# A transformer and RWKV layer stack on one core: the loading block ahead of batch 0 is dissolved into the main block

## The reference

```python
x = x + attn_a(_layernorm(x), Wq, Wk, Wv, Wo)      # 16 heads of 16, rotary, causal softmax
x = x + ffn(_layernorm(x), w_gate, w_up, w_down)   # weights int32 / 127, hidden 768
x = x + attn_b(_layernorm(x), maa_*, Wr, Wk, ...)  # 4 heads of 64, state S = w*S + k v
x = x + ffn(_layernorm(x), w_gate, w_up, w_down)
```

## Time and profile before

| | us |
|---|---|
| median of 3 runs | 3376.86 (3376.3 to 3377.62) |
| profiled execution, its own time | 3373.62 |
| span of the profiled execution | 3371.8 |
| TensorE matmul busy | 2943.3 (87%) |
| VectorE busy | 2399.7 (71%) |
| ACT, GpSimd busy | 1311.6 (39%), 1413.6 (42%) |
| granted TensorE clock, mean | 0.960 |

### The profile page before, as it was taken

One profiled execution on the slowest core, in us unless ns is written; L12 is line 12 of the kernel. 1 busy time (PEld: TensorE's weight loads), 2 busy tenths in 40 slices (PEclk: granted clock), 3 DMA queues, 4 the chain that ended last, 5 costly groups with the idle time before them and its releaser, 6 DMA issues.

```text
span 3371.8 us, 47013 instructions
## 1 busy us (share of the span) xinstructions
PE 2943.3 (87%) x17088; PEld 1831.6 (54%) x17088; DVE 2399.7 (71%) x4593; ACT 1311.6 (39%) x2721; POOL 1413.6 (42%) x1596
## 2 busy tenths in 40 slices
PE   2398989989899898999989998898988989899898
PEld 1135565365653666445763457635575365654567
DVE  4485687767877677866778658785587756876666
ACT  0164314723246323453225532364313733247222
POOL 0123462335623356234552336423463334623454
PEclk9699999999999999999999999999999999999999
DMA  3700024000340004300051002500024000240000
GB/s 132 129 2 1 19 39 96 2 1 19 46 89 2 1 19 69 66 2 10 17 89 39 1 10 41 102 2 2 19 39 96 2 1 19 39 84 2 1 1 14
DMA packets 70610, 114.96 MB, mean 34 GB/s; under 512 B 9451, under 2 KB 62731, under 8 KB 64187
## 3 DMA queue, kind: packets, MB, share of 16 engines
q1 hardware_dynamic: 67091, 110.72, 16.8%
q10 hardware_dynamic: 3264, 0.79, 0.1%
HBM read 74.69 MB, written 33.65 MB: 32 GB/s over the span
## 4 chain that ended last, share of the span: by engine, by line
PE 51%; DVE 23%; POOL 12%; issue 5%; ACT 3%; DMA 3%; SPq 0%; DVEq 0%; POOLq 0%; ACTq 0%
PE PB L1411 7%; PE PB L1395 6%; PE PB L1381 6%; PE PB L1483 5%; PE PB L1468 5%; DVE mxp L1073 4%; DVE arena L1250 4%; PE PB L1420 3%; PE PB L1525 3%; DVE arena L1259 3%; DVE attn L995 2%; PE PB L1560 2%; POOL hl L683 2%; PE PB L1550 2%; DMA arena<-augT 2%
## 5 line engine op out<-in xcount | busy, mean ns | idle before, releaser
L1073 DVE TENSOR_REDUCE mxp<-PB 128x1 f32<-128x512 f32 (+3 forms) x1216 | 723.5, 652 | 149.3 <-PE PB L1384 96.1
L826 ACT ACTIVATE arena<-PB 128x512 f32<-128x512 f32 (+3 forms) x1536 | 657.6, 512 | 408.6 <-PE PB L1395 358.5
L1381 PE MATMUL PB<-arena 96*128 96x512 bf16 (+3 forms) x1536 | 463.2, 343 | 49.4 <-DMA arena<-parts 31.5
L1395 PE MATMUL PB<-arena 99*128 99x512 bf16 (+3 forms) x1536 | 444.1, 336 | 45.1 <-DMA arena<-augT 25.6
L683 POOL TENSOR_TENSOR hl<-arena,hh 128x512 fp32r<-128x512 f32 x192 | 251.8, 1311 | 357.0 <-ACT hh L853 354.0
L1468 PE MATMUL PB<-xh,wgu 128*128 128x512 f32 x768 | 317.1, 413 | 34.0 <-DVE xl L1126 18.4
L1411 PE MATMUL PB<-arena 128*32 128x512 f32 (+3 forms) x3072 | 325.6, 498 | 9.6 <-POOL arena L659 9.6
L1468 PE MATMUL PB<-xl,wgu 128*128 128x512 f32 x768 | 310.0, 404 | 0.6 <-issue 0.6
L1381 PEld LDWEIGHTS PB<-arena 96*128 96x128 bf16 x1536 | 151.6, 100 | 281.0 <-DVE mxp L1073 96.3
L659 POOL TENSOR_SCALAR_AFFINE_SELECT arena<-arena 128x512 f32<-128x512 f32 x256 | 162.4, 635 | 330.8 <-ACT arena L826 304.0
L703 POOL TENSOR_TENSOR arena<-arena,xT 128x512 f32<-128x512 f32 x160 | 184.2, 1175 | 261.8 <-DVE arena L1192 261.8
(11 more groups left out here) (142 smaller groups left out, 5531.1 us busy)
## 6 DMA issues: line engine op xcount, KB each, us to landing
arena<-parts SPq DMA_DIRECT2D x112, 256.0 KB, 9.5
parts<-arena SPq DMA_DIRECT2D x192, 128.0 KB
arena<-parts SPq DMA_DIRECT2D x16, 768.0 KB, 17.4
arena<-in_x SPq DMA_DIRECT2D x16, 512.0 KB, 7.0
arena<-parts SPq DMA_DIRECT2D x16, 512.0 KB, 19.6
xres<-in_x SPq DMA_DIRECT2D x16, 512.0 KB, 4.6
out<-xres SPq DMA_DIRECT2D x16, 512.0 KB, 14.0
wgu<-arena SPq DMA_DIRECT2D x2, 768.0 KB, 4.5
```

Of the source, the lines that this page charges most:

```text
L826: act.activation(pt[:, U % 3, h, 0:n], bank(b, "score", t)[:, 0:n], ACT.Exp, scale=DH ** -0.5).then_inc(act_emptied, 1)
L1073: dve.reduce_max(mxp[:, k // 2 % 2, hs[0]:hs[-1] + 1, col:col + 1], bank(b, "max", t)[:, 0:n * len(hs)].rearrange("p (h n) -> p h n", n=n) ...
L1381: last = mm(ps, qst[0:AUG, i // 4, HG * (k // 2) + h, 128 * (i % 4):128 * (i % 4) + 128], kst[0:AUG, s0 // HALF, HG * (k // 2) + h, 0:n], ...
L1395: mm(ps[:, 0:n], kst[0:AUG + 3, j // 4, h, 128 * (j % 4):128 * (j % 4) + 128], qst[0:AUG + 3, f, h, HALF - n:HALF], start=True, stop=True) ...
```

## The change

There is one block now. SP's order in it: x of batch 0; ident and the q, k, v weights (s_qkv); the rotary tables (s_rope); the three integer matrices and the causal mask (s_ints), now at HIGH in the arena; ones_dram; the parts stores and stack loads of batch 0; then the moves of the feed-forward weights (s_raw), wo in 4 pieces, all other weights (s_w, NLOAD 23 loads); the width row; then as before. GpSimd's memsets stand ahead of its first scale. TensorE waits for s_qkv ahead of its first transpose, and for s_cast (causal and identb) ahead of batch 0's steps. VectorE waits for s_rope ahead of the rotary part; behind the last split of the head it casts the masks and the integers, in place and in three parts, and checks the width part by part, cast, comparison (`not_equal` in place of a subtraction and a comparison with zero) and maximum. ACT waits for s_raw ahead of batch 0's exponentials and their augT DMAs. The flag is made on VectorE behind the third joined maximum of batch 0 and loaded by TensorE at O_STEP. What reads the late weights waits for s_w once, in batch 0.

```diff
-        with nc.Block() as block:
-            @block.sync
...
-                dve.tensor_copy(identb[:, :], ident[:, :]).then_inc(s_cast, 1)
...
+        NW = NC * HID
+        whole = [region(HIGH + NW * k, NW) for k in range(3)]
+        wide_at = rounded("wide_at", HIGH + 3 * NW, [128, 1, NW])
+        wide_col = region(HIGH + 12800, 4)
...
                 x0_in(0)
+                sp.dma_start(ident[:, :], consts[0][:, 0:128]).then_inc(s_qkv, 16)
+                for k, w in enumerate(w_at[0:3]):
+                    sp.dma_start(wqkv[:, :, D * k:D * k + D], w.rearrange("(c p) n -> p c n", p=128)).then_inc(s_qkv, 16)
+                for k in (0, 1):
+                    sp.dma_start(rope[:, k, :], cs[k]).then_inc(s_rope, 16)
...
+                sp.wait_ge(s_zero, NZERO)
+                sp.dma_start(ones_dram, ones).then_inc(s_ones, 16)
                 parts_store(0, range(4))
                 stack_loads(sp, 0, 0)
                 parts_store(0, range(4, 8))
+                sp.wait_ge(s_ones, 16)
                 stack_loads(sp, 0, 1)
+                sp.wait_ge(s_whole, 3)
+                for k in (0, 1):
+                    sp.dma_start(wgu[:, :, HID * k:HID * k + HID].bitcast(f32),
+                                 whole[k].rearrange("p (c n) -> p c n", c=NC)).then_inc(s_raw, 16)
+                sp.dma_start(wd[:, :, :].bitcast(f32), whole[2].rearrange("p (m n) -> p m n", m=NM)).then_inc(s_raw, 16)
...
+                sp.wait_ge(s_wide, 10)
+                sp.dma_start(wide_row[0:1, :], wide_col[:, 3:4]).then_inc(s_flag, 16)
...
+                    if b == 0:
+                        act.wait_ge(s_raw, 48)
                     for t in range(NSC):
...
+                dve.wait_ge(s_rope, 32)
                 for e in (0, 2, 4, 6):
                     pair(rotary, 0, e)
                     pair(remainder, 0, e)
                     pair(low, 0, e)
+                dve.wait_ge(s_ints, 64)
+                dve.wait_ge(s_qkv, 64)
+                dve.tensor_copy(causal[:, :], causal_in)
+                dve.tensor_copy(identb[:, :], ident[:, :]).then_inc(s_cast, 1)
+                for k in range(3):
+                    dve.tensor_copy(whole[k], whole[k].bitcast(i32)).then_inc(s_whole, 1)
+                dve.wait_ge(s_whole, 3)
+                w_ = wide_at[:, 0, :]
+                for k in range(3):
+                    if k:
+                        dve.wait_ge(s_wide, 3 * k)
+                    dve.tensor_copy(w_, whole[k]).then_inc(s_wide, 1)
+                    dve.wait_ge(s_wide, 3 * k + 1)
+                    dve.tensor_tensor(w_.bitcast(f32), whole[k], w_.bitcast(f32), ALU.not_equal).then_inc(s_wide, 1)
+                    dve.wait_ge(s_wide, 3 * k + 2)
+                    dve.reduce_max(wide_col[:, k:k + 1], w_.bitcast(f32), axis=AX.X).then_inc(s_wide, 1)
...
+                        if b == 0 and t == BLOCK_END[5]:
+                            dve.wait_ge(s_flag, 16)
+                            dve.reduce_max(wide_row[0:1, 0:1], wide_row[0:1, :], axis=AX.X).then_inc(s_wide, 1)
+                            dve.wait_ge(s_wide, 11)
+                            dve.tensor_copy(wide_flag[0:1, :], wide_row[0:1, 0:1]).then_inc(s_wide, 1)
+                            dve.wait_ge(s_w, 16 * NLOAD)
+                            dve.wait_ge(s_zero, NZERO)
...
-                pe.reg_load(wide, wide_flag[0:1, 0:1])
...
+                pe.wait_ge(s_qkv, 64)
                 for f in (0, 1):
                     transpose_x0(0, f)
...
+                    if b == 0:
+                        pe.wait_ge(s_cast, 1)
                     for t in range(STEPS):
+                        if b == 0 and t == O_STEP:
+                            pe.wait_ge(s_w, 16 * NLOAD)
+                            pe.wait_ge(s_wide, 12)
+                            pe.wait_ge(s_raw, 48)
+                            pe.reg_load(wide, wide_flag[0:1, 0:1])
```

137 lines of the change are left out of this document (55 added, 82 removed).

## The result

| | before | changed |
|---|---|---|
| median, us | 3377.11 (3376.3 to 3377.62) | 3338.73 (3336.75 to 3340.49, 4 runs) |
| profiled execution: span, own time | 3371.8, 3373.62 | 3338.7, 3340.49 |
| first score matmul (L1395, now L1410) | 155.42 | 115.53 |
| from there to the end of the span | 3216.4 | 3223.2 |
| granted clock, mean | 0.960 | 0.957 |

The ratio of the medians is 0.9886 (95% interval 0.9869 to 0.9904): the change saves 38.4 us. The forecast was 3332.4, range 3324 to 3346: sign and range hold, and some 6 us of the forecast gain of 44.5 did not come. The two profiled executions do not stand at the medians: the one before took 3373.62, 3.5 less than its median, and the changed one 3340.49, 1.8 more. So the spans differ by less (33.1) than the medians do (38.4).

What follows compares the result with a forecast made beforehand. It took an initial wall of 53.84 us, then batch 0's head and transfers, to set the first score, with TensorE, VectorE and ACT binding afterwards. -53.1 + 0.5 + 7.2 + 0.5 + 0.4 = -44.5 us gave 3332.4, range 3324 to 3346.

Steps and rivals of the forecast that it cites:

- Step 1: Start of the kernel: SP issues the load of x at 0.78 instead of 53.84, saving 53.06 us.
- Step 2: Batch 0's head: TensorE's first transpose waits for ident and the q, k, v weights, costing 0.5 us.
- Step 3: VectorE's width check behind its last split ends at 66.6, delay falls into TensorE's standstill: cost 0, uncovered 1.2 us.
- Step 4: ACT's first augT DMA waits for the weight moves, then takes 3.0 us: first score at 162.6 instead of 155.42, +7.2.
- Step 5: Batch 0's flag: TensorE's register load costs 0.5 us, VectorE's two one-row operations 0.4 us.
- later stages the same within 1 us each: Expected sign: stages behind the first score keep their lengths within 1 us and shift by about 44.5 us.
- (a): Batch 0's first augT DMA is held as before by queued bulk: 3344 us, at the full 24.30 us 3354; chance 10%.
- (b): Batch 0's head is bound by its loads, at 201 GB/s instead of 314: 3339 us; chance 8%.
- (c): Nothing given back before the first score: moves pass in the crawl, augT is free; 3326 to 3327 us; chance 12%.
- (d): Clock stays low in batch 0 after TensorE's longer standstill: slower, 3414 us at half the stretch; chance 2%.
- (e): Some early wait on the late weights pulls the initial wall back; chance 1%.

Runs made afterwards that it cites:

- stack_loads_split: The change with weight moves ahead of the last two parts stores, ones rows halved, heads 8-15 stack loads split: five behind first augT, four behind second; 3303.29 us.
- split_no_check: stack_loads_split with transposes waiting for the identity alone, and the width check's ten VectorE operations left out; 3302.69 us.
- again: The changed kernel, unaltered, run once more; 3337.44 us.
- augT_first: The change, with SP waiting for the first augT DMA to land before issuing wo and the other late weights; 3333.82 us.
- ones_first: The change, with ones rows of heads 0 to 7 loaded ahead of those heads' stack loads, those of heads 8 to 15 behind the moves; 3331.57 us.
- flag_not_read: The change with the width check's answer not read: TensorE's register gets a zero before the first transpose, VectorE's two flag operations are gone; 3337.82 us.
- moves_in_gap: The change with the three weight moves placed ahead of the stack loads of heads 8 to 15; 3332.43 us.
- moves_between_one_wait: The change with weight moves ahead of the last two parts stores, ones rows halved, heads 8-15 stack loads waiting for the first augT alone; 3316.21 us.

## Why the prediction was right, and where it was off

**The first question was the right one.** "How much earlier is the first L1395 matmul" decided the result: 39.9 and 39.7 us in the two profiles of the change. The forecast was 45.4 (53.06 less 0.5 and 7.2).

*Step 1, the wall:* 53.06 forecast, 53.05 measured.

*Step 2, the head waits for weights:* +0.5 forecast. The first transpose came at 9.10 with its input ready at 8.15: +0.95, twice the term. It did not last: the first parts store was 0.4 late (22.69, with 22.29 due), and TensorE's first piece for the maxima at 64.02 was early by 0.2. The weights landed 5.70 us after the last issue; in stack_loads_split, the same head, at 10.42, so that this wait varies from one execution to the next by more than its size. The single semaphore of four loads is what exposes it.

*Step 3, the check beside the head:* the first maximum at 67.31, forecast 66.6. The comparisons and maxima of a third took 1.75 where a third of L508 and L512 is 1.65, and gaps between them came with it. Cost 0, and for a better reason than the one given: in split_no_check augT is not held up by transfers, and leaving the check out still gains nothing.

*Step 4, the new wait on ACT:* +7.2 forecast, and this is the step that was mis-sized. Steps 2 and 4 together were 7.7 and measured 13.2 (and 13.4 in again). Two terms of step 4 make up the 5.5. The moves were done at 108.40 (108.85 in again), forecast 107.0. The crawl of the ones rows was there as read, 0.52 MB of the moves passed in it as forecast, and the rest ran at the forecast 400 GB/s: by 105.25 all but 11 rows were through. The sum had no term for the tail, in which these last rows took until 107.66. It is 3 us long with the ones rows ahead and late weights beside it, shorter without the weights (augT_first, last row at 106.42), and gone in ones_first. And augT took 7.08 and 6.91, forecast 3.0, bound 6: the upper bound was too near. "Near the free one", because 1 KB rows turn over faster, was the wrong inference. The rate beside it was higher indeed (248 GB/s against 128), but the share was 1.10: the engines were as full, and augT waited, 5.05 us to its first packet where a free one waits 1.5 (augT_first). augT_first shows the price: with the weights held back it takes 2.36. The total stayed in its range because no other term was off by much, not because this one was bounded well.

*Step 5, the flag:* +0.9 forecast; nothing that flag_not_read can tell, 3337.8 against 3337.4 and 3338.7.

*The rest:* "later stages the same within 1 us each" is not what the profiles show. The rest was 2.8 and 6.8 us longer in the two profiles of the change than in the first of the kernel before, in batch 0 above all, and the prediction's own sentence would call that wrong. But most of it is the spread between executions: by the medians 1.2 to 1.5 us are left, where step 5 had 0.9. The cause of what is left is open.

So the forecast gain of 44.5 becomes, by the medians, 53.05 - 13.2 - 1.5 = 38.4 in the first runs and 53.05 - 13.4 - 1.2 = 38.5 in again; the last term of each is what the median leaves, not a measurement of its own. Nearly all of the missing 6 us is step 4.

**The rivals.** (a) augT held: the fact lies between the forecast and this rival's weak form; augT took 4.1 us over the forecast, not 12. The prediction says that the trace does not tell the rule of the Trainium skill (DMA: Bandwidth & Descriptors, section "Queues, rings and completion order") from waiting for turns. The packet records do. In the kernel before augT is issued at 131.07, its first packet moves at 142.0, the other 47 of them are strewn over the next 12 us among SP's packets, with none from 149.2 to 153.0, while the three packets of ones rows run (149.0 to 153.3); the last ends at 153.7, and the increments follow within 0.2 us. In moves_in_gap, moves_between_one_wait and the change the first packet moves 9.7, 9.3 and 5.05 us behind the issue, with the engines free 1.4 to 1.5. So it is the data that waits for its turn. From the increments to the landing it is then 0.6 to 0.7 us with the engines free and 1.2 to 2.2 beside bulk: only in this last part, up to 1.6 us, could the rule's wait for earlier writes lie, and no run here shows whether it does.

(b) fell: the first parts store came at 22.69, not 30. (c) fell: 0.52 of the 2.36 MB passed in the crawl, as forecast, and augT was not free. (d) fell: the clock was back at 0.94 within 120 to 125, after a standstill of 35.24 us. The rule of the Trainium skill (TensorE: Matmul & The Clock Gate, section "The HAM clock gate") has the full clock return after sustained work and names no condition on the pause before it; the trace agrees. (e) fell: x was issued at 0.79.

## What to carry to other kernels

When a setup block is dissolved into the first iteration, its transfers join a queue that this iteration lives on; the gain is then set by the order on that queue, and further changes to that order and its waits were worth nearly as much (35 to 38 us) as the change itself (38). Sort the queue by who waits: a tiny transfer on which a whole stage stands (augT) should find the engines empty, so hold bulk loads back on its semaphore, and fill the time that this leaves with a counted part of the bulk. And before crediting the removal of one wait, look for the other transfer that ends at about the same time: moves_in_gap ended a wait 24 us earlier and won 5 to 6. And before a difference between two profiles is explained, look where their executions lie among all the others of the same kernel: both profiles of the kernel before fell at the low end of a spread of 10 us.

## What the runs showed of the hardware

- The same 12 KB DMA on ACT's queue took 2.24 to 2.51 us with the engines free of bulk, 6.91 to 7.55 beside the late weights at a share of 1.10, 14.86 beside the last of the stack loads and late weights (143 GB/s, share 1.03), and 24.30 to 25.94 beside the whole of the stack loads (128 to 138 GB/s, share 0.94 to 1.06). Most of that is time in which none of its 48 packets of 256 B has moved (1.4 to 1.5 us free; 5.05 to 5.14, 9.3 and 9.7 to 11.5 in the other cases) or in which they move one by one among SP's.
- A DMA of three partitions (96 KB) went as three packets of 32 KB, 4.1 to 4.6 us each. In that time the rate was 103 GB/s with the engines full, 3 KB packets beside them took 443 ns instead of 126, and what stood behind it came 4.5 to 5 us later than with the rows placed elsewhere in packets of 8 KB, where the same stretch ran at 277 GB/s.
- A transfer issued first does not keep the engines for itself: the move of wd, issued at 66.94, landed at 84.69 (17.75 us for 768 KB, where it took 6.3 in the kernel before with only the other two moves beside it), with stack loads issued from 71.32 on beside it.
- TensorE's register load in mid-stream and two one-row VectorE operations had no price that these runs can tell.
- Ten VectorE operations (some 14 us) less ahead of the first maxima gained nothing: TensorE, at a mean clock of 0.58 to 0.66 over 60 to 72 us after its wait for stack loads, set that place.
